# Attention scores from float32 queries and keys in row strips, in place of bfloat16 parts stacked through DRAM

## The reference, cut to what matters

```python
x: (4, 1024, 192)                                  # 4 images ("batches") b
h = relu(pointwise(depthwise_conv7(x)))            # along the 1024 tokens
h = maxpool2(h)                                    # 512 tokens
h = layernorm(real(fft2(h)))                       # 512 x 192
# attention, 12 heads of 16, on layernorm(h)
q, k, v = hn @ Wq.T, hn @ Wk.T, hn @ Wv.T
q, k = taylor_exp(q), taylor_exp(k)                # so that q.k = 1 + s/4 + (s/4)**2/2
h = h + (causal(q.k) @ v / causal_sum(q.k)) @ Wo.T
# one-expert-of-8 feed-forward on layernorm(h), a tridiagonal solve per image, output
```

## Time and profile before

| | us |
|---|---|
| median of 3 runs | 442.74 (440.92 to 443.55) |
| span of the profiled execution, first to last instruction | 438.5 |
| PE busy | 386.0 (88%) |
| DVE busy | 277.3 (63%) |
| ACT busy | 161.5 (37%) |
| POOL busy | 82.0 (19%) |

### The profile page before, as it was taken

One profiled execution on the slowest core, in us unless ns is written; L12 is line 12 of the kernel. 1 busy time (PEld: TensorE's weight loads), 2 busy tenths in 40 slices (PEclk: granted clock), 3 DMA queues, 4 the chain that ended last, 5 costly groups with the idle time before them and its releaser, 6 DMA issues.

```text
span 438.5 us, 7785 instructions
## 1 busy us (share of the span) xinstructions
PE 386.0 (88%) x2592; PEld 264.3 (60%) x2593; DVE 277.3 (63%) x890; ACT 161.5 (37%) x310; POOL 82.0 (19%) x121
## 2 busy tenths in 40 slices
PE   6999899799898999899998999597999999998273
PEld 4576557234655337553387437486989999997251
DVE  5588844896868998788145283516446556566783
ACT  1001130685205854058532593035333534433000
POOL 1000000270001610016000157402312212111100
PEclk8999999899989999999997599959999999999555
DMA  8587049300691005800059915521621121213504
GB/s 267 163 281 256 0 137 261 94 2 19 177 249 50 1 16 165 217 0 2 18 157 222 365 69 198 176 37 32 170 56 42 50 56 42 63 37 63 162 0 144
DMA packets 33331, 49.52 MB, mean 113 GB/s; under 512 B 15269, under 2 KB 29285, under 8 KB 31701
## 3 DMA queue, kind: packets, MB, share of 16 engines
q1 hardware_dynamic: 29908, 44.40, 35.7%
q0 software_dynamic: 1872, 3.88, 2.6%
q10 hardware_dynamic: 1520, 0.86, 0.7%
HBM read 38.93 MB, written 12.49 MB: 117 GB/s over the span
## 4 chain that ended last, share of the span: by engine, by line
PE 52%; DVE 23%; DMA 7%; ACT 7%; issue 5%; POOL 4%; SPq 2%; DVEq 0%; ACTq 0%; POOLq 0%
PE att L1533 9%; PE ring L1519 7%; PE ring L1523 4%; DVE wide L778 4%; PE ring L1392 4%; PE att L1404 4%; PE ring L1325 3%; ACT probs L642 3%; DMA w1b<-k_parts 3%; POOL tokens_by_expert L593 2%; PE att L1376 2%; PE att L1450 2%; PE misc L1443 2%; PE ring L1300 1%; DVE x2T L877 1%
## 5 line engine op out<-in xcount | busy, mean ns | idle before, releaser
L583 POOL TENSOR_SCALAR_AFFINE_SELECT probs<-probs 128x256 f32<-128x256 f32 (+1 forms) x72 | 41.0, 572 | 220.7 <-ACT probs L642 220.5
L642 ACT ACTIVATE probs<-ring,ones 128x1024 f32<-128x1024 f32 (+2 forms) x72 | 66.5, 971 | 13.0 <-PE ring L1392 11.5
L1533 PE MATMUL att<-w,probs 128*128 x276 | 50.7, 335 | 3.4 <-DVE probs L1060 3.4
L1533 PEld LDWEIGHTS att<-w,probs 128*128 128x128 f32 x276 | 45.9, 196 | 4.2 <-issue 3.9
L1392 PE MATMUL ring<-w1b 128*128 128x512 bf16 (+3 forms) x192 | 40.5, 321 | 6.5 <-ACT probs L642 3.5
L778 DVE SCALAR_TENSOR_TENSOR wide<-w,wdw,wide 128x512 f32<-128x512 f32 x60 | 43.8, 773 | 0.9
L1404 PE MATMUL att<-probs,va 128*32 128x512 f32 (+3 forms) x384 | 40.0, 454 | 1.6 <-POOL probs L583 1.1
L602 POOL DMA_INDIRECT ffn_by_token<-probs,target x23 | 23.2, 1010 | 76.7 <-DVE probs L1067 76.1
L1392 PEld LDWEIGHTS ring<-w1b 128*128 128x128 bf16 x192 | 12.9, 100 | 38.5 <-ACT probs L642 27.2
L732 ACT ACTIVATE probs<-ring,q_area 128x128 f32<-128x128 f32 x72 | 19.9, 376 | 29.5 <-DVE k_area L1043 18.8
L1060 DVE TENSOR_TENSOR probs<-att,oT 128x192 f32<-128x192 f32 x23 | 8.2, 358 | 35.4 <-PE att L1533 33.9
(11 more groups left out here) (315 smaller groups left out, 692.7 us busy)
## 6 DMA issues: line engine op xcount, KB each, us to landing
w1b<-q_parts SPq DMA_DIRECT2D x16, 384.0 KB, 5.6
w1b<-k_parts SPq DMA_DIRECT2D x16, 384.0 KB, 9.3
w<-in_w SPq DMA_DIRECT2D x1, 4608.0 KB, 14.8
w1a<-in_w1a SPq DMA_DIRECT2D x1, 3072.0 KB, 11.2
q_parts<-q_area SPq DMA_DIRECT2D x24, 96.0 KB, 2.1
k_parts<-k_area SPq DMA_DIRECT2D x24, 96.0 KB, 2.1
tokens_by_expert<-in_empty_rows SPq DMA_DIRECT2D x1, 2254.0 KB, 11.1
probs<-tokens_by_expert SPq DMA_DIRECT2D x23, 96.0 KB, 2.2
```

The source lines that it names most:

```text
L583: nc.gpsimd.affine_select(diag, diag, [[0, len(UNITS[n][1])], [1, P]], ALU.is_ge, minus_one, base=0, channel_multiplier=-1).then_inc(p_rea ...
L642: nc.scalar.activation(squares(n), bank[:, :, 0:N - P * j], ACT.Square, bias=ones[:, 0:1], scale=0.25).then_inc(sq_done, 1)
L1533: last = nc.tensor.matmul(att[2][:, 0:D], hT[slot][:, c, :], w2[:, bass.ds((e * HC + c) * D, D)], start=(c == 0), stop=(c == HC - 1))
```

## The change

q and k stay float32. The parts, the DRAM buffers, the stacks, their 20 transfers per image and the VectorE and ScalarE work on them are gone. The projection writes q and k so that each head has 16 rows at the start of a strip of 32 partitions (`wqk` is padded to 128 columns per group of four heads), and a score matmul contracts these 16 rows: heads 4g to 4g+3 use row strips 0 to 3 of the array. A unit is now two heads and one block, or the blocks j = 2 and 3 side by side (256 + 128 columns), so there are 18 units again, of 1024 or 768 columns. Two units are issued one after the other, then the values of the pair before them; head groups are finished one at a time, and `att` uses two banks. ScalarE copies the sums of a group inside attend. Channels are cut 128 + 64 in place of 96 + 96: the 64-row remainders of the two token halves sit in the two halves of the array. `conv` is 1024 contiguous tokens, one instruction per tap; for images 2 and 3 the whole convolution stands in front. The load of w1b (1536 KB), whose space the stacks shared, moves from behind attend(3) to the start.

```diff
-GROUPS = [pair_units(0, g) for g in range(HG)]
-for g in range(HG):
-    GROUPS += [[(j, tuple(range(4 * g, 4 * g + 4)))] for j in (3, 2)] + [pair_units(1, g)]
+BLOCKS = (((0, 0),), ((1, 0),), ((2, 0), (3, N // 2)))
+UNITS = [(g, blocks, pair) for g in range(HG) for blocks in BLOCKS for pair in range(2)]
...
@@ ScalarE attend
+                    if n > PER_GROUP and n % PER_GROUP == 3:
+                        sums(b, n // PER_GROUP - 1)
+                sums(b, HG - 1)
...
@@ ScalarE project: parts out, copies in
-                    nc.scalar.activation(part[0][:], ring[r][0:DC, :, :], ACT.Copy).then_inc(ready1, 1)
-                    act.wait_ge(rest_ready, b + 1)
-                    nc.scalar.activation(part[1][:], rest, ACT.Copy).then_inc(ready2, 1)
+                for r in range(HG):
+                    act.wait_ge(qk_done, HG * b + r + 1)
+                    nc.scalar.activation(qk[:, 2 * r:2 * r + 2, :].rearrange("p i (h n) -> p i h n", h=2),
+                                         ring[(r + 1) % 2][:, :, :].rearrange("p h (i n) -> p i h n", i=2),
+                                         ACT.Copy).then_inc(qk_copied, 1)
...
@@ VectorE front and project
-                    convolve(b + 1, (0,))
+                    convolve(b + 1)
-                    nc.vector.tensor_tensor(rest, src[0:DC, :, :], part[0][:], ALU.subtract
-                    nc.vector.tensor_tensor(part[2][:], rest, part[1][:], ALU.subtract).then_inc(ready3, 1)
-                    if b < B - 1:
-                        convolve(b + 1, (1,))
...
@@ TensorE project
+                for r in range(HG):
+                    for h in range(2):
+                        for i in range(2):
+                            nc.tensor.matmul(out[:, h, 2 * P * i:2 * P * i + 2 * P], wqk[:, 0, 2 * r + i, :],
+                                             xT_long[:, 2 * P * h:2 * P * h + 2 * P], start=(i == 0), stop=False)
+                    for i in range(2):
+                        for h in range(2):
+                            last = nc.tensor.matmul(out[:, h, 2 * P * i:2 * P * i + 2 * P],
+                                                    wqk[rows_of(h), 1, 2 * r + i, :], xT_short[rows_of(h), :],
+                                                    start=False, stop=(i == 1))
+                    if r == 1 and b > 0:
+                        turn_attended(b - 1)
...
@@ TensorE attend
-                pe.wait_ge(s_stack, 16 * STACK_LOADS * (b + 1))
+                pe.wait_ge(qk_copied, HG * (b + 1))
-                        last = nc.tensor.matmul(bank[:, at, 0:N - P * j],
-                                                k_stack[:, h, P * j:P * j + P], q_stack[:, h, P * j:N],
+                    for j, at in blocks:
+                        for i, head in enumerate(unit_heads(n)):
+                            rows = slice(QUAD * (head % 4), QUAD * (head % 4) + HD)
+                            last = nc.tensor.matmul(bank[:, i, at:at + N - P * j],
+                                                    qk[rows, HG + g, P * j:P * j + P], qk[rows, g, P * j:N],
+                for n in range(0, NU + 2, 2):
+                    if n < NU:
+                        scores(n)
+                        scores(n + 1)
+                    if n > 0:
+                        values(n - 2)
```

More of the change, by code:

```diff
@@ L1338, in project @@
+                pe.wait_ge(qk_copied, HG * b + 2)
+                by_tile([ring4[0][:, i, 0:D] for i in range(NT)], xT, wv, v_done)
+                if b > 0:
+                    pe.wait_ge(qk_copied, HG * b + 3)
                     turn_back(b - 1)
@@ new lines, in by_tile @@
+            def by_tile(out, chunks, w, done):
+                for i in range(NT):
+                    nc.tensor.matmul(out[i], chunks[:, P * i:P * i + P], w[:, 0, :], start=(i % 2 == 0), stop=False)
+                for i in (0, 2, 1, 3):
+                    rows, at = rows_of(i // 2), N + P * (i % 2)
+                    last = nc.tensor.matmul(out[i], chunks[rows, at:at + P], w[rows, 1, :],
+                                            start=False, stop=(i % 2 == 1))
+                last.then_inc(done, 1)
@@ L1372, in output @@
+            def turn_back(b):
+                pe.wait_ge(o_ready, 2 * b + 2)
+                turned_chunks(back_ring(b), att_tok, back_done)
             def output(b):
                 pe.wait_ge(back_copied, b + 1)
-                for i in range(NT):
-                    for c in range(2):
-                        last = nc.tensor.matmul(projected[:, i // 2, i % 2, :], att_T[:, c, P * i:P * i + P],
-                                                wo[:, c, :], start=(c == 0), stop=(c == 1))
@@ L1378, in output @@
-                last.then_inc(wo_done, 1)
+                by_tile([projected[:, i // 2, i % 2, :] for i in range(NT)], att_T, wo, wo_done)
             def attend(b):
-                pe.wait_ge(s_stack, 16 * STACK_LOADS * (b + 1))
+                pe.wait_ge(qk_copied, HG * (b + 1))
+                sets = 2
                 def scores(n):
-                    j, heads = UNITS[n]
-                    bank = (ring if len(heads) == 2 else ring4)[n % 2]
+                    g, blocks, _ = UNITS[n]
+                    bank = score_bank(b, n)
@@ L1395, in scores @@
                     last.then_inc(s_done, 1)
                 def values(n):
-                    j, heads = UNITS[n]
+                    g, blocks, _ = UNITS[n]
                     if n == 0 and b > 0:
                         pe.wait_ge(attn_added, b)
-                    pe.wait_ge(p_ready, NU * b + n + 1)
-                    for at, h in enumerate(heads):
-                        g, q = divmod(h, 4)
-                        last = nc.tensor.matmul(att[g][QUAD * q:QUAD * q + QUAD, P * j:N],
-                                                va[:, j, h, :], squares(n)[:, at, :],
-                                                start=(j == 0), stop=(j == 1))
@@ L1407, in values @@
-                    last.then_inc(av_done, 1)
-                first = [sum(len(group) for group in GROUPS[:i]) for i in range(len(GROUPS) + 1)]
-                for n in range(NU + 2):
+                    if n == 2 * PER_GROUP:
+                        pe.wait_ge(ot_copied, HG * b + 1)
+                    pe.wait_ge(p_ready, NU * b + n + 2)
+                    for j, at in blocks:
+                        for u in (n, n + 1):
+                            for i, h in enumerate(unit_heads(u)):
+                                q = h % 4
+                                last = nc.tensor.matmul(att[g % 2][QUAD * q:QUAD * q + QUAD, P * j:N],
+                                                        va[:, j, h, :], squares(u)[:, i, at:at + N - P * j],
+                                                        start=(j == 0), stop=(j == 3))
```

259 lines of the change are left out of this document (98 added, 161 removed).

## The result

The changed kernel takes 501.43 us (median of 4 runs, 500.74 to 503.85), the kernel before 443.14 in the same comparison (440.92 to 445.97): a ratio of 1.133 (95% interval 1.126 to 1.139), 58 us slower. The forecast was 448.8 with a range to 455.5. The profiled execution spans 499.5 us where before spanned 438.5: 61.0 us more.

The account below looks back on a forecast made before the run. The prediction took TensorE in turn with the two score buffers as the new bound: four attends +13.05 us, the rest -6.95, total +6.1, so a 444.6 us span, plus 4.2 to the median: 448.8 us, range 442 to 455.5.

Parts of the forecast that it names:

- In every attend but parts of two the clock is 1.00: Attends: TensorE's granted clock read from the kernel before; the new loop was walked with a lower clock only in attend(3).
- the rival that the clock falls: Attends: scores on a quarter of the array's rows lower the clock; 33.8 us per attend, near 490 us; chance 0.06.
- The loop's own price: Attend: TensorE in turn with the two buffers takes 23.1 us per attend, 25.1 in attend(3).
- the 0.86 that I took for its stream: Scores in attend: 512 float32 columns stream in 0.86 us, so a unit of block 0 costs 0.86.
- Units serialise: Scores in attend: a strip's matmul is held until the other unit's is through; 453 us; chance 0.10.
- ScalarE keeps the pace: Attend: both units of a pair stream at once, about 20.35 us per attend, 437 to 438 us; chance 0.13.
- all in front: VectorE's whole convolution, 13.5 us, stands in front, done some 7 us before turn_attended ends.
- Between the attends: From one attend to the next: 32.85 us, against 36.50 and 34.83 before.
- the turn: TensorE in project: 0.1 us per change of tiling, giving 2.75 us per q and k round and 2.1 for v.
- the waits for the stacks and for the convolution: Ahead of attend(0) and in pointwise: the 2.02 us stack wait goes, and no wait for VectorE ahead of pointwise(2) and (3).
- the sum: Start of attend(0): 1.5 us earlier, from no wait for the stacks and project(0) 0.5 us longer.
- Behind attend(3) nothing moves: The stretch after attend(3) was forecast unchanged, at 173.1 us.

Follow-up runs that it names:

- run 1: Kernel before, each bfloat16 score matmul contracting only the first 16 rows of the stacks; 485.6 us, ratio 1.097.
- run 2: Kernel before, each bfloat16 score matmul over all 128 rows issued twice; 463.0 us, ratio 1.045.
- run 3: Changed kernel, each score matmul contracting the whole strip of 32 rows, rows 16 to 31 zeros; 469.5 us, ratio 1.060.
- run 12: Changed kernel with scores over 32 rows and 32 tiny instructions more at ScalarE's start; 460.7 us, ratio 1.048.
- run 7: Kernel before with the contiguous convolution whole in front and channel chunks of 128 and 64 rows; 447.6 us, ratio 1.010.
- run 8: Kernel before with the channel chunks of 128 and 64 rows alone, convolution as before; 437.6 us, ratio 0.997.

## Why the prediction was wrong

**The step that failed** is the clock: "In every attend but parts of two the clock is 1.00", taken over to a loop whose scores contract 16 rows, with 0.06 for the rival that the clock falls and nothing of it in the range. Runs 1, 2 and 3 show it from three sides: 16 rows in bfloat16 lose the clock, double streams over 128 rows keep it, and zeros in rows 16 to 31 mostly bring it back. The rival was priced about right: 33.8 us per attend at the lower clock, measured 34.0, 32.4, 32.3 and 36.0, and near 490 in all for 501. Some 30 us of the 61 or more are the clock's: the attends sum to 134.65 us in the changed kernel and to 104.96 in run 12, which still had 0.94 in attend(0) and 0.76 in attend(3).

The Trainium skill's "TensorE: Matmul & The Clock Gate", section HAM oscillation — how this bites in real kernels, sums the rule up as "no PE-idle gaps" beyond a length that it gives. By that rule this loop, in which TensorE's waits in attend(1) are one of 0.41 and one of 1.04 us, should have kept its clock. Here page and measurement differ, and the measurement decides: the clock stayed down through 27 us in which TensorE was busy for 96%.

**The loop's own price** was mis-sized a little: 23.75 us at clock 1.00 for 23.1 in attend(2). The start times of single records, in four narrow cuts of TensorE's timeline of that attend (two units of 512 columns, two strips each, two records to a matmul):

```profile
206.11 0.70 PE L1363 MATMUL ring<-qk 32*128 32x512 f32 x2
...
206.64 0.59 PE L1363 MATMUL ring<-qk 32*128 32x512 f32 x2
...
206.90 0.70 PE L1363 MATMUL ring<-qk 32*128 32x512 f32 x2
...
207.43 0.59 PE L1363 MATMUL ring<-qk 32*128 32x512 f32 x2
```

A matmul's second record starts 0.53 us after its first, where half of the 0.86 that I took for its stream is 0.43. So a unit of 512 columns costs 1.06 us and not 0.86, which the earlier trace rows showed already: there too the successor starts after 1.06. The second unit starts 0.79 us behind the first, 0.27 before the first's records would be through one after the other. **Units serialise** is thus excluded, and **ScalarE keeps the pace** didn't happen: two units overlap by a quarter, and not whole, and attend(2) takes 23.75 us where that rival needed 20.35.

In attends (0) and (1) it is 25.4: VectorE's contiguous convolution now lies beside the selects, and they slow down. In run 3's attend(0), GpSimd's and VectorE's timelines:

```profile
92.87 0.65 POOL L558 TENSOR_SCALAR_AFFINE_SELECT probs<-probs 128x256 f32<-128x256 f32 x1 [0.95 <-ACT probs L615]
93.88 3.53 POOL L558 TENSOR_SCALAR_AFFINE_SELECT probs<-probs 128x256 f32<-128x256 f32 x3 [0.35 <-ACT probs L615]
```

```profile
93.72 8.70 DVE L745 SCALAR_TENSOR_TENSOR wide<-w,wdw,wide 128x1024 f32<-128x1024 f32 x8
```

Three selects take 3.53 us, 1.18 each for some 0.5. The forecast costed the convolution at nothing there ("all in front"), and didn't ask who runs beside it. That these selects are slow because of VectorE is read from timelines of runs 3, 7 and 8; I made no run that moves the convolution alone in the changed kernel.

**Between the attends** the prediction said 32.85 us; at clock 1.00 it is 34.31, in run 3 (TensorE's timeline of project(2)):

```profile
169.08 1.99 PE L1277 MATMUL ring<-xT,wqk 128*128 128x256 f32 x8
...
172.07 0.61 PE L1310 MATMUL upper<-pref,sel 128*128 128x204 f32 x2
...
179.12 1.57 PE L1331 MATMUL ring<-wv,xT 128*128 128x192 f32 x8
...
181.46 0.66 PE L1321 MATMUL ring<-ident,probs 128*128 128x128 f32 x4
```

A round of q and k takes 2.99 us for 2.75 (169.08 to 172.07), v 2.34 for 2.1. In both, the part over 128 rows and the part over 64 rows each take 0.2 us more than their streams (a round 1.92 and 1.07 for 1.72 and 0.86), where 0.1 was taken for the turn. In the changed kernel the first 3.5 us of the stage are at the lower clock, and it takes 35.7. Ahead of attend(3) the stage takes 36.91 for 33.4: its mean clock of 0.82 is 13.3 us at the lower level, before (0.89) it was 7.3, and that accounts for some 3 of the 3.7 us. That the waits for the stacks and for the convolution go was right: scores start at 76.14 with none ahead, and pointwise starts directly behind the prefix. The start came 3.3 us earlier and not 1.5, because the first transposes already come at 45.59 for 48.00, which the sum had at nothing. The change doesn't explain that: image 0's convolution takes 8.7 us for 8.9. TensorE's first 14 matmuls of 512 columns begin at 7.46 for 8.64, the load that they wait for having landed earlier, and last 6.54 us for 7.90, at a clock of 1.00 for 0.81 (means of 7.46 to 13.84 and of 8.64 to 16.38). Run 2, with project and front of the kernel before, had these matmuls at 7.79 with 6.54 us and its first transposes at 46.05. The drop of the clock there stands in six of the seven traces with bfloat16 scores and in none of the nine with float32 scores; why it is missing in these, and why the loads land earlier, no run tried.

**Behind attend(3) nothing moves** was wrong by 7.25 us. TensorE's two waits there are 6.3 us together, where before has one of 0.46 in that place, and with 32 rows the stretch takes 180.7 us with ScalarE's wait (run 3) and 173.2 without (run 12), as before (173.1). So the wait accounts for it; what causes the wait is the open question above.

## What to carry to other kernels

Before scores or any hot matmul are cut to fewer rows, ask what the clock does: a matmul that streams as long over 16 rows as over 128 is no lighter for the schedule, but here it cost half the clock for 27 of the 32 us of an attend, and padding with zero rows, free in streams, gave 32 of the 58 us back. Look at the granted clock beside the busy share: 96% busy at 0.50 is a slow engine, not a full one. And of work that is moved to an idle stretch, ask which engine runs beside it there.

## What the runs showed of the hardware

- In these loops the clock followed the rows of the array that take part, not what they hold: means of 0.51 to 0.59 in attends (0) to (2) with 16 rows in bfloat16, 1.00 in attends (1) and (2) with 128 (even when streamed twice), and per attend 0.50 to 0.58 with strips of 16 rows, 0.79 to 1.00 with strips of 32 (half of them zeros, run 3).
- With 64 rows one loop ran at either level in one execution: 29.1 and 31.0 us at 0.53 and 0.50, 19.8 and 19.8 us at 1.00. Down once, 1.3 us into attend(0), the clock stayed down for 27.3 us.
- Selects on GpSimd took 1.1 to 1.2 us each beside VectorE's three-operand instructions over 1024 contiguous columns, 0.54 to 0.84 beside those over 512 interleaved ones, and mostly 0.41 to 0.64 ahead of them.
- ScalarE sat 10.3 to 15.5 us ahead of a copy while GpSimd's 12 scatters ran, in some kernels and in others not. In seven of them it went on 1.7 to 2.1 us after the last scatter had ended.
